# Score matmuls on the 32 partitions of one head, two heads in turn, in place of zero-padded queries

## What is computed

```python
x: (8, 100, 512)   ctx: (8, 722, 512)   N_HEADS = 16, HEAD_DIM = 32
qh = split(layernorm(x) @ Wq + bq); kh = split(ctx @ Wk + bk); vh = split(ctx @ Wv + bv)
scores = einsum('bhqd,bhkd->bhqk', qh, kh) * 32 ** -0.5
attn = sparsemax(scores)                  # clip(scores - tau, 0), tau by a sorted prefix sum
x = x + einsum('bhqk,bhkd->bhqd', attn, vh).reshape(8, 100, 512) @ Wo + bo
h = layernorm(x)
x = x + sqrt((h @ cos(theta + theta_noise)) ** 2 + (h @ sin(phi + phi_noise)) ** 2)
```

## Time and profile before

| | |
|---|---|
| median of 3 runs | 843.59 us (840.98 to 843.95) |
| profiled execution | 843.08 us, span 840.8 us |
| mean granted clock of TensorE | 0.886 of 2.4 GHz |
| PE matmuls busy | 657.9 us, 78% |
| DVE busy | 629.0 us, 75% |
| ACT busy | 454.7 us, 54% |
| POOL busy | 181.9 us, 22% |
| score matmuls | 768, busy 151.7 us |

### The profile page before, as it was taken

One profiled execution on the slowest core, in us unless ns is written; L12 is line 12 of the kernel. 1 busy time (PEld: TensorE's weight loads), 2 busy tenths in 40 slices (PEclk: granted clock), 3 DMA queues, 4 the chain that ended last, 5 costly groups with the idle time before them and its releaser, 6 DMA issues.

```text
span 840.8 us, 16547 instructions
## 1 busy us (share of the span) xinstructions
PE 657.9 (78%) x4960; PEld 423.0 (50%) x4960; DVE 629.0 (75%) x4046; ACT 454.7 (54%) x872; POOL 181.9 (22%) x147
## 2 busy tenths in 40 slices
PE   3796824778887779898888979997759979995485
PEld 2463613644466445664467536744447446742351
DVE  3699994699936997599929993899629994999401
ACT  2262745554486454874498438854538447842441
POOL 5710530002420034202420152015300152000000
PEclk9898765889889789999899989998979989997698
DMA  9610100000020000200020002000020000000000
GB/s 311 231 49 1 72 1 1 3 2 0 11 92 1 0 11 1 92 0 0 10 93 0 0 10 92 1 0 10 1 91 0 0 10 13 3 1 10 11 2 10
DMA packets 9806, 26.25 MB, mean 31 GB/s; under 512 B 2090, under 2 KB 2090, under 8 KB 8686
## 3 DMA queue, kind: packets, MB, share of 16 engines
q1 hardware_dynamic: 9710, 25.35, 8.7%
HBM read 23.71 MB, written 1.64 MB: 30 GB/s over the span
## 4 chain that ended last, share of the span: by engine, by line
DVE 70%; issue 10%; PE 8%; DMA 5%; DVEq 3%; SPq 2%; ACT 2%; ACTq 0%
DVE cand L743 22%; DVE cand L755 17%; DVE top L750 14%; DMA xq<-in_x 3%; DVE csum L765 2%; PE work L333 2%; PE work L338 2%; PE tps L406 2%; DMA out_y<-att 2%; DVE topz L761 2%; DVE gk L768 1%; SPq L193 1%; DVE g_max L771 1%; DVE st L718 1%; DVEq L830 1%
## 5 line engine op out<-in xcount | busy, mean ns | idle before, releaser
L743 DVE MAX8 cand<-S 100x8 f32<-100x60 f32 (+1 forms) x1536 | 191.0, 205 | 43.5 <-issue 25.4
L406 PE MATMUL tps<-ident,S 100*128 100x100 f32 x768 | 102.9, 276 | 80.6 <-DVEq L835 46.6
L390 PE MATMUL work<-kT,qz 128*100 128x361 f16 x768 | 151.7, 339 | 0.8 <-ACT k_f L565 0.8
L581 ACT ACTIVATE S<-S,neg_tau 100x722 f32<-100x722 f32 x128 | 114.3, 895 | 69.8 <-DVE neg_tau L773 69.8
L755 DVE MATCH_REPLACE8 cand<-top,cand 100x96 f32<-100x96 f32 x640 | 148.1, 243 | 0.0
L750 DVE MAX8 top<-cand 100x8 f32<-100x96 f32 x768 | 139.9, 245 | 0.0
L333 PE MATMUL work<-ctxT,wk 128*128 128x361 f16 x768 | 134.1, 340 | 7.0 <-ACT k_f L565 5.7
L406 PEld LDWEIGHTS tps<-ident,S 100*128 100x128 f32 x768 | 84.7, 155 | 101.2 <-ACT pT L546 44.0
L283 POOL TENSOR_TENSOR ctxT<-ctxT_f,ctxT 128x1024 f16<-128x1024 f32 (+1 forms) x24 | 46.8, 1950 | 393.1 <-ACT ctxT L546 392.8
L333 PE MATMUL work<-wv,ctxT 128*128 128x512 f16 x576 | 125.7, 379 | 0.4 <-ACT S L546 0.4
L546 ACT ACTIVATE S<-work 100x722 f32<-100x722 f32 x128 | 99.4, 776 | 27.9 <-PE work L390 25.4
(11 more groups left out here) (99 smaller groups left out, 586.5 us busy)
## 6 DMA issues: line engine op xcount, KB each, us to landing
ctxT_f<-in_ctx SPq DMA_DIRECT2D x8, 1444.0 KB, 6.7
xq<-in_x SPq DMA_DIRECT2D x8, 200.0 KB
xr<-in_x SPq DMA_DIRECT2D x8, 200.0 KB
out_y<-att SPq DMA_DIRECT2D x8, 200.0 KB
wq<-in_L_xattn_Wq SPq DMA_DIRECT2D x1, 1024.0 KB, 9.2
S<-in_L_xattn_Wk SPq DMA_DIRECT2D x1, 1024.0 KB, 11.5
S<-in_L_xattn_Wv SPq DMA_DIRECT2D x1, 1024.0 KB, 10.8
wcos<-in_L_ffn_theta SPq DMA_DIRECT2D x1, 1024.0 KB, 12.8
```

Source lines behind the costliest of these rows:

```text
L390: last = nc.tensor.matmul(buf[0:L, half, 0:HALF], qz2[:, i, h // G, h % G, :], kT2[:, j, h // G, half * HALF:(half + 1) * HALF], start=(n ...
L406: last = nc.tensor.transpose(tps[:, half, c * L:(c + 1) * L], S[0:L, h, kc * P:(kc + 1) * P], ident[0:L, 0:L])
L581: nc.scalar.activation(S[0:L, h, 0:N], S[0:L, h, 0:N], ACT.Relu, bias=neg_tau[:, h:h + 1], accum_out=row_sum[:, h:h + 1]).then_inc(relu_do ...
L743: last = nc.vector.max(cand[:, j, 8 * i:8 * i + 8], S[0:L, h, cuts[i]:cuts[i + 1]])
```

## The change

The zero-padded copies go. The queries stay as they lie, in `qT2`, and a score matmul reads the 32 partitions of its head on both sides. `scores` is called for every second head, takes both slots, and issues the matmuls of the two heads in turn, twelve in all; it raises `work_full` by two on the last of them. Its wait asks that both slots be empty. POOL's nine instructions become three over 128 partitions.

```diff
-        qz2 = sb("qz2", [P, 2, DC, G, L], F16)
+        qT2 = sb("qT2", [P, 2, DC, L], F16)
...
-            pool.memset(qz2[:, :, :, :, :], 0.0).then_inc(const_ready, 1)
-            pool.wait_ge(const_ready, 3)
...
-            def pad_q(b):
...
+            def split_q(b):
+
+                bias = bq_c[:, :].rearrange("p (m a) -> p m a", a=1).broadcast_to([P, DC, L])
                 pool.wait_ge(q_raw_ready, 2 * (b + 1))
-                for j in range(G):
-                    r = slice(DH * j, DH * (j + 1))
-                    pool.tensor_tensor(qz2[r, 0, :, j, :], q_raw[r, :, :],
...
+                pool.tensor_tensor(qT2[:, 0, :, :], q_raw[:, :, :], bias, ALU.add).then_inc(qT_ready, 1)
+                pool.wait_ge(qT_ready, 2 * b + 1)
+                pool.tensor_tensor(q_raw[:, :, :], q_raw[:, :, :], bias, ALU.add).then_inc(q_sum, 1)
                 pool.wait_ge(q_sum, b + 1)
...
+                pool.tensor_tensor(qT2[:, 1, :, :], q_raw[:, :, :], qT2[:, 0, :, :],
+                                   ALU.subtract).then_inc(qT_ready, 1)
+                pool.wait_ge(qT_ready, 2 * b + 2)
...
             def scores(b, h):
+
                 if h % G == 0:
                     pe.wait_ge(k_lo_ready, DC * b + h // G + 1)
 
-                if h < 2:
-                    pe.wait_ge(k_f_ready, DC * (b + 1) - 1 + h)
+                if h == 0:
+                    pe.wait_ge(k_f_ready, DC * (b + 1))
                 else:
-                    pe.wait_ge(s_ready, H * b + h - 1)
-                buf = take()
+                    pe.wait_ge(s_ready, H * b + h)
+                m = h // G
+                bufs = (take(), take())
                 for half in range(2):
                     for n, (i, j) in enumerate(((0, 0), (0, 1), (1, 0))):
-                        last = nc.tensor.matmul(buf[0:L, half, 0:HALF], qz2[:, i, h // G, h % G, :],
-                                                kT2[:, j, h // G, half * HALF:(half + 1) * HALF],
-                                                start=(n == 0), stop=(n == 2))
-                last.then_inc(work_full, 1)
+                        for head, buf in zip((h, h + 1), bufs):
+                            r = slice(DH * (head % G), DH * (head % G + 1))
+                            last = nc.tensor.matmul(buf[0:L, half, 0:HALF], qT2[r, i, m, :],
+                                                    kT2[r, j, m, half * HALF:(half + 1) * HALF],
+                                                    start=(n == 0), stop=(n == 2))
+                last.then_inc(work_full, 2)
...
-                        scores(b, G * g + j)
+                        if j % 2 == 0:
+                            scores(b, G * g + j)
```

More of the change, by code:

```diff
@@ L149, in build_kernel @@
         ctx_lo_ready, k_lo_ready = sem("ctx_lo_ready"), sem("k_lo_ready")
-        xT_ready, q_raw_ready, qz_ready = (sem(n) for n in ("xT_ready", "q_raw_ready", "qz_ready"))
+        xT_ready, q_raw_ready, qT_ready = (sem(n) for n in ("xT_ready", "q_raw_ready", "qT_ready"))
         v_ready = sem("v_ready")
@@ L258, in _ @@
             pool.wait_ge(bq_scaled, 1)
-            def pad_q(b):
+            def split_q(b):
+                bias = bq_c[:, :].rearrange("p (m a) -> p m a", a=1).broadcast_to([P, DC, L])
                 pool.wait_ge(q_raw_ready, 2 * (b + 1))
-                for j in range(G):
-                    r = slice(DH * j, DH * (j + 1))
-                    pool.tensor_tensor(qz2[r, 0, :, j, :], q_raw[r, :, :],
[L266 to L271, removed]
-                pool.wait_ge(q_sum, b + 1)
[L273 to L277, removed]
+                pool.tensor_tensor(qT2[:, 0, :, :], q_raw[:, :, :], bias, ALU.add).then_inc(qT_ready, 1)
+                pool.wait_ge(qT_ready, 2 * b + 1)
+                pool.tensor_tensor(q_raw[:, :, :], q_raw[:, :, :], bias, ALU.add).then_inc(q_sum, 1)
+                pool.wait_ge(q_sum, b + 1)
+                pool.tensor_tensor(qT2[:, 1, :, :], q_raw[:, :, :], qT2[:, 0, :, :],
+                                   ALU.subtract).then_inc(qT_ready, 1)
+                pool.wait_ge(qT_ready, 2 * b + 2)
             def low_ctx(b, i):
@@ L296, in prepare @@
                     low_ctx(b, i)
-                pad_q(b)
+                split_q(b)
                 for m in range(DC):
@@ L455, in ffn_of @@
                 project(buf[0:L, 1, :], lambda c: x2T[:, c, :], lambda c: wsin[:, c, :]).then_inc(work_full, 1)
-            pe.wait_ge(const_ready, 3)
+            pe.wait_ge(const_ready, 2)
             xT_of(0, take()).then_inc(work_full, 1)
@@ L469, in one_pass @@
             def one_pass(b, first, last):
-                pe.wait_ge(qz_ready, 2 * G * (b + 1))
+                pe.wait_ge(qT_ready, 2 * (b + 1))
                 for g in range(DC):
```

## The result

The changed kernel took 866.22 us (median) beside 843.77 us for the kernel before, a ratio of 1.026 with an interval of 1.020 to 1.032. The forecast was 846.1 us, with a range of 841.5 to 858. The profiled execution has a span of 863.6 us against 840.8, that is 22.8 us more.

The account below looks back on a forecast made before the run. DVE's chain was taken to bound the kernel, with PE's scores mostly off the path. Terms 0.9 + 0.7 + 0.7 - 0.4 + 0.8 + 0.2 + 0.1 = +3.0 us on 843.1 gave 846.1 us, range 841.5 to 858.

Parts of the forecast that it names:

- What bounds the kernel: Whole kernel: DVE's chain sets the time; halving PE's scores, about 9 us per pass, gains nothing except in the first group.
- Side by side: Score matmuls: two heads on different partitions run together, twelve matmuls in 1.1 to 1.4 us; the rival without it had 0.15.
- The edges: Between score matmuls and transposes: one exposed tail with extra weight loads, 0.2 us per pair, +0.8 over passes 3 to 6.
- The first group: First four heads of a pass: pair waits and low clock delay s3, the fourth copy; passes 3 to 6: +0.9, +0.7, +0.7, -0.4.
- pass 7: Start of pass 7, without ln1: DVE waits for a flag sum now behind the first score pair, +0.2 us (bounds 0 and 1.5).
- The rest of a pass: Later groups: 0.9 us longer in groups 1 and 2, stage end 2 to 3 us later, hidden by 6.02 us of PE idle.
- a rival at 10% and 858 us: Whole score stage: the clock falls because PE is busy less, overfilling idle time by 2 to 3 us per pass; chance 0.10.
- POOL: POOL's query copies: about 6 us less work per pass, worth 0 (bounds 0 to -1.1, from pass 0 beside a DVE scan).

Follow-up runs that it names:

- the last two kernels: Changed kernel with head pairs on 64 partitions and GpSimd waiting for DVE's third threshold group: 845.2 us; the same with the first group as before: 845.63 us.
- POOL's wait: Pairs on 64 partitions, plus GpSimd's last low part of the next context waiting for DVE's third threshold group in looped passes: 845.2 us, ratio 1.001.

## Why the forecast was wrong

*What bounds the kernel*: right. PE's score time was worth nothing, as the last two kernels show.

*Side by side*: right, 1.13 us for twelve against 1.1 to 1.4. The Trainium skill's statement ("TensorE: Matmul & The Clock Gate", Packing small matmuls), that row groups run at the same time, holds here for two groups of 32 and of 64 partitions: in 1.13 us twice the work of the 1.09 us in the earlier trace rows. The edges, forecast with the weight loads at 0.2 us a pair, took 0.26 us (0.12 and 0.14).

*The first group*: right in mechanism, and near in size for passes 3 to 5. The starts of passes 3, 4 and 5 came 1.06, 0.87 and 0.81 us later (0.9, 0.7 and 0.7 with 0.2 each for the edge were forecast), pass 6 0.61 earlier (0.4 less the edge, so 0.2), pass 7 0.26 later (0.2). Pass 2 came 0.60 us earlier, for which nothing was forecast. PE was idle for 2.36 us ahead of T2 and then had the low clock through T2, S23 and T3.

*The rest of a pass*: this step failed. It said "The pair's wait makes a group of heads some 0.9 us longer in groups 1 and 2" and "hidden". At full clock a group grew by 0.5 us (7.8 us with pairs of 64, against 7.3). But in the changed kernel it took 10.4 us, since the clock fell in every one. The score stage of pass 4 ended some 10 us later, not 2 to 3, and 6.02 us of idle time could not hide that. I had this as a rival at 10% and 858 us, and my ground against it was that "outside the first group the new gaps are below 1 us each". The gaps were indeed short. They did not matter: with gaps as long the 64-partition pairs kept the clock, and without any gaps the single 32-partition heads lost it. Both the low chance and the rival's own reason, that "PE is then busy less of the time", came from taking busy time alone for what holds the clock. No row of the kernel before had a matmul that contracts over fewer than 100 partitions, so nothing there could show the difference; I should have counted that unknown as one, as I did for side-by-side.

*POOL*: a second term put at nothing. The work that it lost (138.0 us busy, 181.9 before) brought no gain, as said. But I missed that ACT's lateness moves POOL's context subtraction onto DVE's scan and the instructions around it. With a like collision in pass 7 it costs 0.9 to 1.9 us in a pass, and together nearly half of the loss in the middle. It does not need the low clock in groups 1 to 3: the pairs on 64 partitions paid it too. The scan of the earlier trace rows was the sign of it, and so were the 1.52 us of the earlier trace rows, which should have been 0.15: I used them only as a bound for a gain and for pass 7.

The parts, by the medians: 64 partitions in place of 32, with the pairing kept and POOL's copies back, -17.5 us (866.2 to 848.7); POOL's wait -3.4 (to 845.2), with overlapping intervals of the ratios; what is left over the kernel before (843.9 in that round) is 1.4 us, inside the noise. These medians come from different rounds and chips. How the clock weighs partitions is not settled beyond the cases run: 32 single, 32 in pairs, 64 single, 64 in pairs, 128. Four heads of 32 partitions side by side were not tried, since the two PSUM slots don't hold them. So it stays open whether the clock asks for many partitions at work at once, or whether matmuls on 32 partitions count for less however many lie side by side.

## What to carry to other kernels

Before narrowing a matmul, ask what holds PE's clock: here the narrow matmuls took the clock from the transposes and the mix beside them, and that cost more than the scores saved. If a contraction must be narrow, lay neighbours so that together they cover all partitions; that is shown here for two of 64. An engine that is "hidden" has a reserve in microseconds; price each way in which it could double, and look what the shifted instructions will then run beside.

## What was not expected of the hardware

- The granted clock does not follow busy time alone: 39.09 of 40 us busy at 0.50 with scores on 32 partitions; 20.40 of 27 us busy at 1.00 with pairs on 64.
- Zero queries on three quarters of the partitions didn't keep the clock down: in the kernel before it was 1.00 over groups 1 to 3. With those partitions left out, one head at a time, it was 0.50 for 40 us.
- Matmuls that nobody reads, in the gaps, made the changed kernel 10 us faster (866.2 to 856.1).
- A DVE scan of 0.56 us took 2.05 us beside a POOL subtraction of 1.73 us, and a DVE subtraction of 0.36 us took 1.81 beside one of 1.72.
